# Step sizes of a state-space layer: Softplus in one ScalarE pass in place of relu, exp, ln and a VectorE maximum

## The reference

```python
xz = x @ Wi.T + bi
x_in, z = xz[..., :512], xz[..., 512:]
xc = causal_conv4(x_in) + conv_b
u = silu(xc)
dt = softplus(x_in[..., :32] @ Wdt.T + bdt)
A = -exp(A_log)
# step by step in time, for each channel and state
h = h * exp(dt * A) + dt * Bm * u
y = sum_n(h * Cm)
out = (y * silu(z)) @ Wo.T + bo + x * Dv.mean()
```

## Time and profile before

| | us |
|---|---|
| median of 3 runs | 771.6 |
| lowest and highest | 767.12, 772.82 |
| the profiled execution, first to last instruction | 761.0 |
| busy: VectorE | 668.2 |
| busy: TensorE (matmuls) | 638.2 |
| busy: ScalarE | 602.9 |
| busy: GpSimd | 309.7 |

### The profile page before, as it was taken

How to read it: one execution, slowest core, us unless ns; L and a number is a source line. 1 busy time by engine, 2 the same in 40 slices (tenths; PEclk the granted TensorE clock), 3 DMA queues, 4 the chain that set the end, 5 groups by cost and what they waited for, 6 DMA issues and landing times. The chain is left out here.

```text
span 761.0 us, 8267 instructions
## 1 busy us (share of the span) xinstructions
PE 638.2 (84%) x2912; PEld 329.6 (43%) x2912; DVE 668.2 (88%) x449; ACT 602.9 (79%) x1066; POOL 309.7 (41%) x189
## 2 busy tenths in 40 slices
PE   7867787799887999978889999967858997874958
PEld 5632333364342465544334673622413654241726
DVE  2437948779999999999999999999999999999691
ACT  2488896879798989998888989898879787855454
POOL 0107020034436497669960866076940150600030
PEclk9997998999998999999999999997978999896979
DMA  8431465341839070523566240705171605205001
GB/s 290 151 138 44 164 226 162 143 161 60 301 92 311 13 249 1 206 71 116 178 232 221 92 158 28 249 0 221 28 238 40 225 24 199 78 28 221 1 0 56
DMA packets 40026, 103.08 MB, mean 135 GB/s; under 512 B 4080, under 2 KB 13040, under 8 KB 39984
## 3 DMA queue, kind: packets, MB, share of 16 engines
q1 hardware_dynamic: 37424, 94.40, 34.0%
q10 hardware_dynamic: 2560, 8.14, 4.6%
HBM read 23.08 MB, written 4.19 MB: 36 GB/s over the span
## 5 line engine op out<-in xcount | busy, mean ns | idle before, releaser
L1097 ACT ACTIVATE G<-RD,COL 128x1024 f32<-128x1024 f32 (+1 forms) x288 | 280.0, 1042 | 61.1 <-PE Y L1386 54.6
L1219 DVE TENSOR_TENSOR_SCAN G<-G,STT,RV 128x1024 f32<-128x1024 f32 (+1 forms) x160 | 313.0, 2018 | 5.7 <-ACT G L1097 5.7
L1219 DVE TENSOR_TENSOR_SCAN G<-G,RV 128x1024 f32<-128x1024 f32 (+1 forms) x128 | 268.7, 2155 | 11.9 <-ACT G L1097 11.9
L1386 PE MATMUL Y<-G,RW 128*32 128x512 f32 x1024 | 142.6, 674 | 61.4 <-DVE G L1219 57.7
L831 POOL TENSOR_SCALAR LV<-LV 128x4 f32<-128x4 f32 x19 | 17.0, 896 | 295.1 <-ACT XN L918 294.8
L1386 PEld LDWEIGHTS Y<-G,RW 128*32 128x32 f32 x1024 | 27.5, 115 | 142.0 <-DVE G L1219 80.2
L857 POOL TENSOR_SCALAR XN<-X,LV 128x256 f32<-128x256 f32 x38 | 86.0, 2267 | 2.0
L1353 PE MATMUL MB<-XI,DIAG 128*64 128x512 f32 x248 | 63.1, 646 | 12.6 <-DMA XI<-XI 10.7
L840 POOL TENSOR_TENSOR LV<-LV,HALF 128x4 f32<-128x4 f32 (+1 forms) x25 | 48.1, 1922 | 62.5 <-DVE LV L1174 60.9
L1312 PE MATMUL MB<-MT,XF 128*128 128x256 f32 x240 | 60.3, 396 | 13.2 <-ACT MT L960 7.6
L871 POOL TENSOR_SCALAR X<-X,LV 128x256 f32<-128x256 f32 x32 | 71.0, 2228 | 0.8
(11 more groups left out here) (93 smaller groups left out, 772.1 us busy)
## 6 DMA issues: line engine op xcount, KB each, us to landing
RD<-DW SPq DMA_DIRECT2D x60, 512.0 KB, 3.8
RV<-DW SPq DMA_DIRECT2D x60, 512.0 KB, 4.8
W<-in_w SPq DMA_DIRECT2D x48, 256.5 KB, 3.6
XI<-XI ACTq DMA_DIRECT2D x30, 256.5 KB, 5.6
X<-in_x SPq DMA_DIRECT2D x8, 512.0 KB, 6.3
out<-X SPq DMA_DIRECT2D x7, 512.0 KB, 3.2
G<-in_w SPq DMA_DIRECT2D x4, 513.0 KB, 8.3
RV<-in_w SPq DMA_DIRECT2D x4, 513.0 KB, 12.2
```

Source lines behind the costliest of these rows:

```text
L1097: eng.activation(G[:, i % NG, t0:t1], RD[:, q, t0:t1], ACT.Exp, scale=NAC[:, states(i):states(i) + 1]).then_inc(sems["exp"])
L1219: eng.tensor_tensor_scan(g, g, RV[:, (4 * k + q) % NR, t0:t1], STT[:, idx:idx + 1] if goes_on else 0.0, ALU.mult, ALU.add).then_inc(sems[" ...
L1386: ins = eng.matmul(Y[32 * q:32 * q + 32, 512 * h:512 * h + 512], RW[:, states(i + o), :], G[:, (i + o) % NG, 512 * h:512 * h + 512], start ...
```

## The change

Softplus is taken from ScalarE's own table set `softplus`. The stages `dtr`, `dte`, `dtl` and VectorE's `dt` go, and with them the constants TOPC and HIGH. In their place are `softset`, a table load, and `dt`, one ScalarE pass for each half of 512 tokens from PSUM to DW row 0, with the bias as a column. They stand in `proj(k)` ahead of `silu`: `dm` follows `um`, then `softset`, `dt`, `zm`, `silu`, `u`, `z`, `expset`. `dts(k)` keeps only XD's making, once in four blocks. In `half`, `softset` and `dt` follow `um`, and `repd` is issued before silu in both halves. The PSUM banks of `dm` are freed by each half of `dt`, the rule that gave `dm` two neighbouring banks goes, and `w` and `repd` wait for both halves of `dt`.

```diff
@@ LOAD
-        "z": (0, 30), "dtr": (0, 25), "dte": (0, 48), "dtl": (0, 48), "silu": (0, 57), "expset": (0, 57),
+        "z": (0, 30), "dt": (0, 30), "softset": (0, 57), "silu": (0, 57), "expset": (0, 57),
@@ def hold
-        if stage == "dm" and item[0] not in HALVED:
...
@@ def dts(k):
-        yield from after(("xtc", 6 * it + 2, 1), ("xtc", 6 * it + 3, 1), ("repd", k - 1, 3, passes(k - 1) - 1))
-        if k % 4 == 0:
-            for hf in range(2):
-                yield 1
-                do("xdm", it, hf)
-                yield 0
-                do("xd", it, hf)
-        yield from after(("w", k - 1, passes(k - 1) - 1))
-        yield 2
+        yield from after(("xtc", 6 * it + 2, 1), ("xtc", 6 * it + 3, 1), ("dt", k - 1, 1))
         for hf in range(2):
-            do("dm", k, hf)
-        yield 0
-        for hf in range(2):
-            do("dtr", k, hf)
-        do("dte", k, 0)
-        yield 0
-        do("dtl", k, 0)
-        yield from rest_for(REST)
-        do("dt", k, 0)
+            yield 1
+            do("xdm", it, hf)
+            yield 0
+            do("xd", it, hf)
@@ def proj(k):
         do("um", k, 0)
         yield 1
         do("um", k, 1)
-        if zs:
-            if zs[0] >= NZ:
-                yield from after(("opm", (zs[-1] - NZ) // 4, 1, 3))
-            yield 2
+        yield from after(("xd", it, 1), ("repd", k - 1, 3, passes(k - 1) - 1), ("w", k - 1, passes(k - 1) - 1))
+        if zs and zs[0] >= NZ:
+            yield from after(("opm", (zs[-1] - NZ) // 4, 1, 3))
+        yield 2
+        for hf in range(2):
+            do("dm", k, hf)
+        yield 0
+        do("softset", k, 0)
+        for hf in range(2):
+            do("dt", k, hf)
+        for ko in zs[:1]:
             for hf in range(2):
-                do("zm", zs[0], hf)
-        yield 0
+                do("zm", ko, hf)
         do("silu", k, 0)
...
         yield from rest_for(REST)
-        yield from after(("dt", k, 0))
         do("w", k, 0)
@@ def half(k, hf):
         do("dm", k, hf)
-        do("dtr", k, hf)
-        do("dte", k, hf)
-        do("dtl", k, hf)
         yield 1
         do("um", k, hf)
+        do("softset", k, hf)
+        do("dt", k, hf)
+        for q in range(4):
+            do("repd", k, q, hf)
         if hf == 0:
-            do("dt", k, hf)
-            for q in range(4):
-                do("repd", k, q, hf)
             yield 0
...
@@ the scans' loop
-            until("dt", k + 1, 0)
+            until("dt", k + 1, 1)
@@ ScalarE
-                    eng.activation(DW[:, 0, 512 * hf:512 * hf + 512], bank("dm", k, hf), ACT.Relu, scale=-1.0,
-                                   bias=TOPC[:, k % 4:k % 4 + 1]).then_inc(sems["dtr"])
...
-                    eng.activation(d, d, ACT.Exp, scale=-1.0, bias=HIGH[:, 0:1]).then_inc(sems["dte"])
...
-                    eng.activation(d, d, ACT.Ln, bias=1.0).then_inc(sems["dtl"])
+                elif stage == "softset":
+                    eng.preload_act_table_set("softplus")
...
+                    eng.activation(DW[:, 0, 512 * hf:512 * hf + 512], bank("dm", k, hf), ACT.Softplus,
+                                   bias=COL[:, BDT + k % 4:BDT + k % 4 + 1]).then_inc(sems["dt"])
@@ VectorE
-                        ins = eng.scalar_tensor_tensor(out=d, in0=o, scalar=COL[:, BDT + k % 4:BDT + k % 4 + 1], in1=d,
-                                                       op0=ALU.add, op1=ALU.max)
-                    ins.then_inc(sems["dt"])
```

More of the change, by code:

```diff
@@ L159, in __call__ @@
         if stage in EMPTIES:
-            self.hold(stage, item, EMPTIES[stage], (item[0], item[1] * (item[0] in HALVED)) if stage == "dm" else item)
+            self.hold(stage, item, EMPTIES[stage], item)
         for b in range(BANKS):
@@ L199, in do @@
         elif stage in FREES:
-            taken[0] -= 2 if stage == "dt" and item[0] not in HALVED else 1
+            taken[0] -= 1
         elif stage == "mm" and item[0] % 8 == 0:
@@ L418, in half @@
         do("expset", k, hf)
-        if hf:
-            for _ in range(HREST[0]):
-                yield 0
-            do("dt", k, hf)
-            for q in range(4):
-                do("repd", k, q, hf)
-        for _ in range(HREST[2] if hf else 1):
+        for _ in range(HREST[0] + HREST[2] if hf else 1):
             yield 0
@@ L472, in begin @@
             for ko in range(2, 16):
-                if 16 * k + s == 16 * ko + first[ko % 4]:
+                if 16 * k + s == 16 * ko + first[ko % 4] and (chain is proj or ko % 4 == 0):
                     yield chain(ko)
-        if (k, s) in PLAN["dts1"]:
-            yield dts(1)
         if (k, s) in PLAN["proj1"]:
@@ L519, in schedule @@
         do("wa", n)
-    for stage in ("ones", "half", "calm", "warm", "b2q", "topc", "nae"):
+    for stage in ("ones", "half", "calm", "warm", "b2q", "nae"):
         do(stage)
@@ L666, in build @@
         HALF = sb("HALF", [P, 4])
-        HIGH = sb("HIGH", [P, 1])
         ZERO = sb("ZERO", [P, 3])
-        TOPC = sb("TOPC", [P, 4])
         RW = sb("RW", [P, 64, 32])
@@ L790, in do @@
                     t0, t1 = span(k, p)
-                    e.wait_ge("dt", k, p)
+                    for hf in halves(k, p):
+                        e.wait_ge("dt", k, hf)
                     e.wait_ge("mm", 15)
@@ L823, in do @@
                 elif stage == "half":
-                    eng.memset(HIGH[:, :], TOP)
                     eng.memset(ZERO[:, :], 0.0)
@@ L1135, in do @@
                     eng.tensor_scalar(DM[:, 1:2], DM[:, 2:3], 1.0 / 512 / 256, None, ALU.mult).then_inc(sems["dmu"])
-                elif stage == "topc":
-                    e.wait_ge("col")
-                    eng.tensor_scalar(TOPC[:, :], COL[:, BDT:BDT + 4], -1.0, TOP, ALU.mult, ALU.add).then_inc(sems["topc"])
                 elif stage == "b2q":
@@ L1158, in do @@
                     ins.then_inc(sems["vmsv"])
-                elif stage == "dt":
-                    k, p = a
-                    e.wait_ge("dtl", k, p)
-                    first = count.bank["dm", (k, halves(k, p)[0])]
-                    wide = len(halves(k, p)) == 2 and count.bank["dm", (k, 1)] == first + 1
-                    for hf in [halves(k, p)] if wide else [[h] for h in halves(k, p)]:
-                        d = DW[:, 0, 512 * hf[0]:512 * hf[-1] + 512]
-                        o = MB[:, first:first + 2, :].rearrange("p a n -> p (a n)") if wide else bank("dm", k, hf[0])
-                        ins = eng.scalar_tensor_tensor(out=d, in0=o, scalar=COL[:, BDT + k % 4:BDT + k % 4 + 1], in1=d,
-                                                       op0=ALU.add, op1=ALU.max)
-                    ins.then_inc(sems["dt"])
                 elif stage == "vvar":
```

16 lines of the change are left out of this document (1 added, 15 removed), and 2 rows, old and new, of the table PLAN.

## The result

| | before | after |
|---|---|---|
| median of 4 runs, us | 771.66 | 827.94 |
| lowest and highest | 767.12, 772.82 | 827.21, 828.03 |
| the profiled execution, us | 761.0 | 826.1 |

A forecast was written before the change was run, and what follows sets the result against it. VectorE was taken to bound the kernel from 165 to 697 us, ScalarE's order before. Terms -2.4 - 16.4 + 0.7 + 2.4 = -15.7 us gave a 745.3 us span, plus 10.6 to the median: 756 us, 8-in-10 range 746 to 769.

The forecast's parts named there:

- The step that failed: PSUM banks of dm: held from s=2 to s=3 instead of some six slots, said only to help others; no cost counted.
- the sum: Whole kernel: start -2.4, maxima of blocks 2 to 14 -16.4, block 6 +0.7, block 14 +2.4, together -15.7 us.
- the one on the slower side: Silu's run: Softplus at its upper bound lengthens it by 3.48 us, exps come late; 778 us, chance 0.10.
- The prices: Per block: Softplus half 0.69 us, table load 1.283, VectorE's maximum 1.258; ScalarE's sum falls 1.0 us, VectorE's total about 21.
- The rule that spoke against the change: ScalarE's table switches: a drain of about 1.38 us each on top of the load would give 764 us.
- Each microsecond taken from it is worth one: VectorE from 165 to 697 us sets the pace alone; 13 maxima of 1.258 us gone give -16.4 us.
- The start: From 40 to 165 us: shorter ScalarE chains let block 1 start 1.5 us earlier and block 2 2.4 us earlier.
- Block 14: TensorE's chain there gains dm, +1.13 us, and scan 12 can't come 1.26 earlier: +2.4 us against the -16.4.
- The first rival: Tight blocks: the longer silu run eats most of the gain; 770 us, or 762 with half given back; 0.20, at 766.
- ScalarE's removed work comes back just ahead of the run: Tight blocks: 3.56 us of relu, exp and ln gone before silu's run offsets 3.8 us of lost margin at scan 8.
- the run's reach: Scan 8 needs the first exp behind silu's run; its margin falls 3.8 us, costing only block 6 +0.7 us.

The follow-up runs named there:

- in_run: Kernel before's list, dm in its old slot, relu, exp, ln and VectorE's maximum replaced by load and Softplus straight ahead of silu; 772.5 us, 1.006 to the kernel before.
- own_slot: Kernel before's list without VectorE's maximum, Softplus where relu stood, with its load and a load back to exp's set; 759.1 us, 0.989 to the kernel before.
- no_max: Kernel before with only VectorE's maximum left out; relu, exp, ln, list and table loads as before; 761.0 us, 0.992 to the kernel before.
- fm_ahead: Kernel before, old arithmetic, with two pairs of FFN matmuls (blocks 5 and 9) moved ahead of the reduction; 785.7 us, 1.026 to the kernel before.

## Why the prediction was wrong, point by point

**The step that failed** is the one that costs what moved: "The banks of `dm` are held from s=2 to s=3 in place of some six slots, which can only help the others", and with it the unspoken one that all other stages keep their slots. The freed banks and the freed share of ScalarE's load put other chains in other slots, and some in worse ones: FFN matmuls ahead of a reduction, copies behind exps. That is 55 us by the medians of the changed kernel and `in_run`, a term that the sum doesn't have. None of the rivals holds it, and the one on the slower side needed a Softplus of its upper price. It could have been seen before any run: the rules of both kernels write their lists without a chip, and a stage that stands on another side of a reduction is plain there.

**The prices were right.** Softplus 0.684 us (0.69 taken), the load 1.283, ScalarE's sum 11.4 us less, VectorE's 18.4 less (20.5 us of maxima went; its other work took 2.1 more). The rule that spoke against the change, the Trainium skill's drain of about 1.38 us for each switch ("ScalarE: Activation LUTs", "What ACT_TABLE_LOAD costs"), does not show here either: in block 9 of `in_run` the load at 509.60 takes 1.28 and Softplus starts at 510.90, with two more such loads behind it in the run.

**"Each microsecond taken from it is worth one"** was wrong by more than half. A share of 528.54 of 532 us says that VectorE was never kept waiting, not that the others had time to spare. Summed over blocks 2 to 14, `own_slot` gains 4.3 us and `no_max` 6.3, of 16.4. Blocks 12 and 13 give 0.8 to 1.2 of their 1.26 in every kernel of the table, block 10 (43.2 to 42.8 in `own_slot`) a third, block 6 nothing.

**The start:** -2.4 forecast, +1.5 came, which one execution each can't tell apart: 162.5 and 167.1 came from one and the same list. Softplus in block 0 ends at 41.8 as forecast (41.6). But for block 1 the chain on ScalarE didn't end at 109.2: `um` waited for its shift DMA until 101.30, not 98.7, `dm` ended at 106.0 and not at 103.5, and the last load at 113.4. In `own_slot` and `no_max` too the start gives nothing that shows (164.5 and 166.9 for 164.6): the 10.2 us at `dt` were the wait for block 1's first inputs, and it moves to `mv`.

**Block 14:** +1.1 forecast, -1.6 came. Scan 12 waited 0.56 us, less than the 1.06 of the earlier trace rows, so `dm` in that chain cost nothing that shows:

```profile
746.87 13.99 DVE L1163 TENSOR_TENSOR_SCAN G<-G,STT,RV 128x1024 f32<-128x1024 f32 x8 [0.56 <-ACT G L1055]
```

**The first rival,** the longer run that eats the gain (766 to 770, 0.20), is what happens once the order is held: `in_run` is at 772.5 and 1.006. I had set against it that ScalarE's removed work comes back just ahead of the run. In block 9 it doesn't (46.8 us for 40.6); in blocks 2, 6, 8 and 10 it does (each 0.8 to 1.3 us shorter than before).

**What I left out** of the run's reach was `w` of blocks 4, 8 and 12, whose silu's run comes late: it waits 6.15, 9.87 and 6.15 us in blocks 3, 7 and 11.

## What to carry to other kernels

Where rules with budgets write the order, an edit to what one chain holds reorders the others: write out both lists and compare them, stage by stage, before any price is put on the edit. On an in-order engine, let nothing that waits for a copy or a DMA stand ahead of the work that frees buffers for another engine; here one such place was worth 8 us. And price the removal of work from a saturated engine by how far the next engine is behind it, not by the engine's share; here a table switch with its pass was better in a slot of its own, at the price of one load more, than in a run that no exp can enter (759.1 us for 772.5).

## What the runs showed of the hardware

A wait of TensorE cost more than its own length here. The granted clock in two stretches of block 9 of the changed kernel, behind the wait of 6.24 us for XF and a little later (columns as in the earlier trace rows):

```profile
524.95:528.60 3.65, 3.65 (x9) 2.90 (x10) 3.65 (x3) 0.01 (x1) 0.00 (x0) 0.50 0.00 0
529.70:533.30 3.60, 3.60 (x25) 1.74 (x23) 0.00 (x0) 0.00 (x0) 0.00 (x0) 1.00 0.00 0
```

```profile
529.69 1.89 PE L1256 MATMUL MB<-MT,XF 128*128 128x256 f32 x8
```

Behind the wait the clock is 0.50 (1.2 GHz), and eight FFN matmuls take 3.78 us; at 1.00 (2.4 GHz) the same eight take 1.89. In the ring of blocks 2, 5 and 9 this lies on the path, since the FFN stands between the copy and the reduction; the first eight take 3.78, 3.46 and 3.78 us there. In block 9 that is 1.9 of the 8.54 us that the exps waited. In `fm_ahead` the same eight took 3.78 as well, at 0.50. It repays to look at what runs first behind a wait.
